# Splitting every second query or key projection of the first phase over two periods, with attention halves and mean products moved behind them

## The reference

```python
Q = (x @ wq + bq).reshape(Bn, Sn, Hn, hd)
K = (x @ wk + bk).reshape(Bn, Sn, Hn, hd)
V = (x @ wv + bv).reshape(Bn, Sn, Hn, hd)
def prep(t):
    h1 = jnp.tanh(jnp.einsum('bshd,do->bsho', t, w1) + b1)
    return jnp.einsum('bsho,on->bshn', h1, w2) + b2
...
qe = jnp.real(jnp.einsum('hcb,bshn->cshn', R, q1))
qq = jnp.sum(qe ** 2, -1)
s = qq[:, :, None, :] * kk[:, None, :, :]
attn = jax.nn.softmax(s / s, axis=2)
out = jnp.einsum('bijh,bjhd->bihd', attn, V).reshape(Bn, Sn, Dn)
return out @ wo + bo
```

## Time and profile before

| | before |
|---|---|
| median of 3 runs | 1529.22 us (1527.8 to 1529.68) |
| the profiled execution | 1528.58 us, span 1526.8 us |
| TensorE busy | 1479.4 us (97%) |
| VectorE busy | 1148.7 us (75%) |
| ScalarE busy | 846.9 us (55%) |
| GpSimd busy | 368.8 us (24%) |

### The profile page before, as it was taken

One profiled execution on the slowest core, in us unless ns is written; L12 is line 12 of the kernel. 1 busy time (PEld: TensorE's weight loads), 2 busy tenths in 40 slices (PEclk: granted clock), 3 DMA queues, 4 the chain that ended last, 5 costly groups with the idle time before them and its releaser, 6 DMA issues.

```text
span 1526.8 us, 28795 instructions
## 1 busy us (share of the span) xinstructions
PE 1479.4 (97%) x11085; PEld 1047.7 (69%) x11085; DVE 1148.7 (75%) x2321; ACT 846.9 (55%) x1123; POOL 368.8 (24%) x404
## 2 busy tenths in 40 slices
PE   9999999999999999999999999999999999999998
PEld 5334343335566666666557888888988888888887
DVE  6545544468999999999967888778786878788676
ACT  5888899866788888888863431322232221222221
POOL 1000000224646666666454300000000000000001
PEclk9999999999999999999999999999999999999999
DMA  7766656457646756656642201100010101110001
GB/s 152 144 112 120 124 99 123 104 87 117 103 68 108 110 74 111 105 81 97 110 143 70 76 15 32 25 28 22 20 30 15 42 14 29 29 29 16 20 22 28
DMA packets 89872, 108.93 MB, mean 71 GB/s; under 512 B 18228, under 2 KB 58176, under 8 KB 89736
## 3 DMA queue, kind: packets, MB, share of 16 engines
q1 hardware_dynamic: 89608, 106.90, 36.9%
q10 hardware_dynamic: 128, 0.20, 0.0%
HBM read 26.29 MB, written 4.19 MB: 20 GB/s over the span
## 4 chain that ended last, share of the span: by engine, by line
PE 73%; DVE 12%; SPq 6%; ACT 3%; issue 3%; DMA 1%; POOL 1%; POOLq 0%; DVEq 0%; ACTq 0%
PE ps L109 70%; SPq L119 6%; DVE NM L1609 2%; PE ps L1382 2%; ACT PX L1550 1%; ACT H L683 1%; DMA XR<-TT 1%; DVE GH L2441 1%; DVE GH L2443 1%; DVE X L2403 1%; DVE TT L2269 1%; PE ps L1344 1%; PE ps L1390 1%; DVE EE L850 1%; ACT GF L2213 1%
## 5 line engine op out<-in xcount | busy, mean ns | idle before, releaser
L1609 DVE TENSOR_REDUCE NM<-ps 128x4 f32<-128x1024 f32 x256 | 307.4, 1220 | 27.3 <-PE ps L109 26.0
L1550 ACT ACTIVATE PX<-ps 128x1024 f32<-128x1024 f32 x256 | 262.2, 1024 | 78.8 <-PE ps L109 77.7
L683 ACT ACTIVATE H<-ps,b1c 128x1024 f32<-128x1024 f32 x256 | 267.6, 1117 | 38.6 <-PE ps L109 37.2
L2213 ACT ACTIVATE GF<-ps,cols 128x512 f32<-128x512 f32 x128 | 87.0, 686 | 257.4 <-PE ps L109 257.4
L109 PE MATMUL ps<-XC,W_sw_w 128*128 128x512 f32 x768 | 187.1, 393 | 0.0
L109 PEld LDWEIGHTS ps<-XC,W_sw_w 128*128 128x128 f32 x768 | 140.0, 188 | 27.6
L2554 POOL TENSOR_SCALAR RSc<-AGc 128x4 f32<-128x4 f32 x23 | 5.6, 243 | 593.9 <-DVE AGc L2328 593.9
L2443 DVE TENSOR_TENSOR GH<-GF,GH 128x512 fp32r<-128x512 f32 x192 | 133.2, 694 | 6.6
L109 PE MATMUL ps<-PX,VT 128*32 128x256 f32 x2048 | 137.1, 385 | 0.1
L2208 ACT ACTIVATE GF<-ps 128x512 f32<-128x512 f32 x64 | 38.1, 596 | 176.2 <-PE ps L109 176.2
L109 PE MATMUL ps<-KT,QT 48*128 48x512 f32 x512 | 127.5, 495 | 2.8 <-DVE NM L1609 1.8
(11 more groups left out here) (254 smaller groups left out, 2507.5 us busy)
## 6 DMA issues: line engine op xcount, KB each, us to landing
KT<-KS SPq DMA_DIRECT2D x128, 192.0 KB, 4.7
ST<-QS SPq DMA_DIRECT2D x254, 96.0 KB, 2.8
QT<-XSb SPq DMA_DIRECT2D x128, 96.0 KB, 4.1
XR<-TT SPq DMA_DIRECT2D x352, 32.0 KB, 1.9
XT<-in_xT_dram SPq DMA_DIRECT2D x8, 512.0 KB, 4.1
raw_a<-in_x_dram SPq DMA_DIRECT2D x8, 512.0 KB, 4.5
CR<-in_ctxT_dram SPq DMA_DIRECT2D x8, 512.0 KB, 4.6
out_dram<-X SPq DMA_DIRECT2D x7, 512.0 KB, 2.9
```

The lines of the kernel that those rows point to most:

```text
L683: e.activation(H1[s % 8][:, :, :], PP[s % 3][:, :, :], ACT.Tanh, bias=b1c[:, half:half + 1], scale=1.0).then_inc(act_th, 1)
L1550: e.activation(PX[s % 3][:, :, :, :], PP[2][:, :, :].rearrange("p g (c q) -> p g c q", c=2), ACT.Exp, bias=0.0, scale=0.25).then_inc(act_e ...
L1609: e.tensor_reduce(NM[u % 2][:, qc, :, :, i], PP[qc][:, :, :].rearrange("p g (m k) -> p g m k", m=2), AX.X, ALU.max, negate=True).then_inc( ...
L2213: e.activation(g[:, :], o, f, bias=cols[:, col:col + 1], scale=1.0).then_inc(act_g, 1)
```

## The change

From J = 35 on, the projection that stands in J = 4n + 3 (J = 35, 39, 43, 47, 51, 55: `halved`) is split. Its first three matmuls (k = 0) stay there, and the last three (k = 1) stand in the next period at the same place, between w1 steps 1 and 2. All that follows from its end moves by one period too: VectorE's two evictions, GpSimd's copy and SP's stack (`projected_due`). To leave bank 7 to the open sum, the rest of the attention halves (J = 40, 48, 56) and the mean product of J = 44 stand behind w2 now, at the end of their period, and the mean vectors of J = 40 and 56 move to the end of J = 41 and 57. On VectorE the reads of these stand behind the projection's eviction.

```diff
+    def halved(J):
+
+        n, t = divmod(J, 4)
+        return t == 3 and n >= DIRECT[0] and n + 2 < NIT
+
+    def projected_due(J):
+
+        if halved(J - 1):
+            return project_due(J - 1)
+        return None if halved(J) else project_due(J)
...
     def means_late_due(J):
-        return {40: 2, 56: 3}.get(J)
+        return {41: 2, 57: 3}.get(J)
...
-        def project(n, c, b, free):
+        def project(n, c, b, free, parts=(0, 1)):
             p, k1 = n // 2, 1 - n % 2
             w.wait_ge(dve_wqk, 4 - 2 * k1)
             w.wait_ge(dve_x, 2 * p + 2)
-            w.wait_ge(*free)
-            for k in range(2):
+            if 0 in parts:
+                w.wait_ge(*free)
+            for k in parts:
...
-            t.then_inc(pe_proj, 1)
+            if 1 in parts:
+                t.then_inc(pe_proj, 1)
...
-            rest = attend_rest_due(J)
-            if rest is not None:
-                free[7] = attend_half(rest, 1, pe_att, free[7])
+            if halved(J - 1):
+                free[7] = project(*project_due(J - 1), 7, free[7], (1,))
...
             if pr is not None and J:
-                free[7] = project(*pr, 7, free[7])
+                free[7] = project(*pr, 7, free[7], (0,) if halved(J) else (0, 1))
...
             m = means2_due(J)
-            if m is not None:
-                b = means2_bank(m)
-                free[b] = means2(m, free[b])
+            if m is not None and means2_bank(m) == 6:
+                free[6] = means2(m, free[6])
...
+            rest = attend_rest_due(J)
+            if rest is not None:
+                free[7] = attend_half(rest, 1, pe_att, free[7])
+            m = means2_due(J)
+            if m is not None and means2_bank(m) == 7:
+                free[7] = means2(m, free[7])
             m = means_late_due(J)
```

More of the change, by code:

```diff
@@ L447, in sync @@
                 dma(e, XM[:, :, :], x_tm[:, 4 * p:4 * p + 4, :], d_xm)
-            pr = project_due(J)
+            pr = projected_due(J)
             if pr is not None:
@@ L828, in centred, with means_rows @@
             t.then_inc(dve_mm, 1)
+        def means_rows(m):
+            w.wait_ge(pe_mb, m + 1)
+            w.wait_ge(pe_att, 2 * m)
+            w.wait_ge(d_bo, 64)
+            e.tensor_tensor(MB[:, :], P[means2_bank(m)][:, 0:256], BO[:, :], ALU.add).then_inc(dve_mb, 1)
         low = P[7][0:48, 0:256]
@@ L856, in vector @@
                     attended(at, u, 6 + u)
-            rest = attend_rest_due(J)
-            if rest is not None:
-                attended(rest, 1, 7)
             if J == SPREAD:
@@ L878, in vector @@
             m = means2_due(J)
[L879 to L884, removed]
+            if m is not None and means2_bank(m) == 6:
+                means_rows(m)
+            pr = projected_due(J)
             if pr is not None:
                 project(*pr, 7)
+            rest = attend_rest_due(J)
+            if rest is not None:
+                attended(rest, 1, 7)
+            m = means2_due(J)
+            if m is not None and means2_bank(m) == 7:
+                means_rows(m)
             if J == BIAS_ROWS:
```

## The result

The changed kernel took **1537.46 us** in the median of 5 runs (1533.82 to 1538.21), the kernel before 1529.22 (1527.8 to 1529.69). The ratio is 1.0049, with a 95% interval of 1.0038 to 1.006: slower by 8.2 us. The forecast was 1528.7 with a range of 1527.0 to 1531.2 and "within 0.2%" at 0.90, so it was wrong in sign and in size. The profiled execution took 1537.66 us.

What follows compares the result with a forecast made beforehand. TensorE was taken to set the pace nearly everywhere. Terms +1.26 - 1.64 - 0.18 + 0.38 + 0 - 0.3 gave -0.5 us, so 1528.1 profiled and a 1528.7 us median, range 1527.0 to 1531.2.

Steps and rivals of the forecast that it cites:

- The mean vector from J=40 to 41: Norms of J=42 may wait for the later centring on VectorE, covered by a 0.27 us stall: counted 0.
- The stacks: Split projections' stacks are issued a period later, but the last still reaches its reader on TensorE in time: 0.
- J=57/58: First maps start 0.98 us earlier in TensorE's work, partly filling J=58's waits, less bank wait and centring: -0.3 us.
- effects further on: Remaining chance of 0.04 for effects further on, making the time either faster or slower.
- A: Rival: halves cost just half of 1.59 us each and waits of J=45 and J=58 are filled: 1526.4 us, chance 0.13.
- B: Rival, slower: the reciprocal in J=43 holds VectorE, delaying the eviction and J=44's mean product; 2.5 us more gives 1531.2, chance 0.13.
- The half projection: Each group of three matmuls takes 0.90 us, so two cost 0.21 more than a whole projection; six splits +1.26 us.
- The stall of J=36: TensorE's 0.82 us wait for ScalarE's tanh is filled by the half projection, also in J=52: -1.64 us.
- The projection of J=41: It waits 0.19 us for VectorE to empty the bank after the attention rest, likewise in J=49: +0.38 us.
- The mean product of J=44: It waits 0.4 us for a late eviction, while J=45's 0.58 us of stalls go: net -0.18 us.

Runs made afterwards that it cites:

- e5: The changed kernel with the projection of J=55 left whole, so the last stack is issued as early as before: 1532.32 us, ratio 1.0023.
- e6: The changed kernel with nine useless matmuls of 128 rows by 512 columns ahead of norms in J=42: 1529.02 us, ratio 1.001.
- e3: The kernel before with only the mean vectors moved to the end of J=41 and 57, nothing split: 1532.13 us, ratio 1.0025.
- e1: The changed kernel with the room for XS doubled, eight columns instead of four: 1529.96 us, ratio 1.0012.
- e7: The changed kernel with both the room for XS doubled and the projection of J=55 left whole: 1528.4 us, ratio 0.9999.
- e10: The kernel before with only the splits of J=35/36 and J=51/52, nothing moved: 1527.56 us, ratio 0.9987.
- e8: The changed kernel with the room for XS doubled and no projection split, the other moves kept: 1531.08 us, ratio 1.0019.
- e9: The changed kernel with one wait added, so GpSimd starts its context tiles only after VectorE's MM: 1531.1 us, ratio 1.0015.
- e4: The changed kernel with useless 48-row matmuls ahead of norms, eight in J=42 and four in J=58: 1533.24 us, ratio 1.0036.
- e2: The changed kernel with the mean vectors back at the end of J=40 and 56: 1533.64 us, ratio 1.0031.

## Why the prediction was wrong

**The step that failed** is "The mean vector from J=40 to 41 ... I count 0, bounds -0.27 and +0.5". The order of VectorE's instructions was read rightly ("behind the eviction, XS and the normalisation of J=41"), but I took XS as ready to run, since in the trace of before it ran directly behind the eviction. It has a wait for the mean vector itself, which the mean vector's old place had always met. The price was 1.99 us for the wait alone (`e5`, `e6`), and 4.64 (8.64 against 4.00) with the fallen clock in the profiled execution. `e3` shows this with that line alone, `e1` by taking it away.

**A second step failed**, "The stacks ... 0" together with J=57/58. I asked whether the late stack would reach its reader on TensorE in time, and it did. What I didn't ask is beside what GpSimd's work would now run. The trace of before had the answer in a row that I used for something else: the gains took 1.23 us and had started at 296.87, 0.06 us behind a GpSimd subtraction (296.81, 1.28 us); in `e7` the same operation started at 296.03, 0.07 us ahead of GpSimd's (296.10), and took 0.22. The Trainium skill ("SBUF — State Buffer", section "Who interferes with whom") states it as a rule: a VectorE instruction with two SBUF inputs contends with a GpSimd instruction that reads SBUF, since its second input comes through a read interface that both share. The rows here agree: 1.68 and 1.86 us beside a subtraction of 1.3 us, 0.52 without. Price 1.33 us, and 3.78 with the clock.

**What was left out altogether** is the granted clock. The forecast added up work and waits at full speed; each of the two waits, of 2.20 and 0.96 us, was followed in the profile by a stretch at half clock that cost 2.65 and 2.45 us more, over half of the loss at both places. A chance of 0.04 "for effects further on" was all I had left for such things. The profiled difference, by first tanhs, comes out as +2.0 (the clock at 42 us, which the kernel before didn't have in its profile), +4.6 (J=42), +3.3 (J=58) and -0.8 for the rest, 9.1 us, so some 7 us of that execution are the change's. The medians differ by 8.2, and the least of the five runs, 1533.82, lies 4.6 above the median of before.

**The rivals.** A (halves free) did not come: groups of three were 0.90 us long throughout (190.60 to 191.50 in `e10`). B named the wrong instruction, the reciprocal in J=43, though the right kind of thing, VectorE held by one wait with the bank's eviction behind it.

**The terms that held**, read in `e7` where nothing ahead disturbs them. The half projection costs 0.90. The stall of J=36 is gone: with both halves counted, J=35 and 36 take 0.63 us less (forecast 0.82 - 0.21 = 0.61). The projection of J=41 waits for X: 0.95 us from w1 to it (216.83 to 217.78), 0.29 more than w1's 0.66, where 0.19 was forecast. The mean product of J=44 was to wait 0.4 us for the eviction behind the reciprocal and waited 0.35. From the first tanh of J=35 to that of J=53 `e7` gained 0.36 us; by the forecast's terms (-1.64, -0.18, +0.38 and five splits at 0.21) it was to be 0.39.

**The term for J=57/58**, "I take -0.3, bounds -0.98 and +0.3", is to be read in `e1`, which has all six splits and no meeting of the two engines. From J=54 to J=59 it took 25.66 us against 25.98 before, 0.32 less; by the forecast's terms, -0.3 and one split at 0.21, it was to be 0.09 less. Part of that is luck: the gains took 0.22 us instead of 1.23, for the reason above, which the forecast did not have. From J=35 to J=63 `e1` gained 0.64 us in its profile, where the forecast's sum says 0.5. `e7` gained nothing from J=35 to J=63: with its last projection whole, the attention rest that was moved leaves a stall of 0.74 us in J=56, as in J=40 of `e8`. So the small terms were right and didn't matter, since two steps that I had set to zero, without looking at the waits behind them, carried the result. That `e7`'s median, 1528.4, is near the forecast of 1528.7 says little, as the kernel before is as near.

**What stays open.** Why the clock falls behind the wait of J=42 in one execution (after, `e3`, `e9`) and not in another with the same instructions (`e5`) was not settled. That it depends on the matmuls ahead is not shown: `e4` and `e6` point that way, but they differ in the number of rows and in the operands, and `e6` kept its clock behind the unfilled wait of J=58 too. Why the median of `e1` is 1.8 us above the kernel before, when its profile is shorter over the changed periods, is open as well. What `e10` would gain with the room for XS doubled as well wasn't run.

## What to carry to other kernels

When an instruction is moved later, list who waits for its semaphore, those that only wait to reuse a buffer too, since in the old trace they wait for nothing and leave no row; then ask what stands behind each of them in its engine's order. A stall that is filled is worth its length at most, so compare it with the price of a new wait, which here was its length plus, in several profiles, as much again or more in fallen clock. Split or move only where the trace has a stall: two splits out of six, with nothing moved, gave the only version whose interval lies below the kernel before.

## What the runs showed of the hardware

- A wait of TensorE of 0.9 to 2.2 us ahead of small groups was followed in several executions by a granted clock of one half: for 6.8 us at 226.8 and at 305.3 (after), for 3.4 us at 219.2 (`e2`) and at 226.2 (`e9`). At half clock w2 takes 3.57 us instead of 1.86. The same wait as at 226.8 left the clock at 1.00 in `e5`, and so did one of 1.14 us in J=58 of `e6`, longer than the 0.96 of the kernel after.
- With eight more matmuls of 48 rows in that wait, which left some 0.9 us of it empty, the clock was 0.50 in the one traced execution, the slowest of five; with nine of 128 rows, which filled it, it was 1.00 in the one traced.
- Part of the spread between executions of one kernel goes with this: the five of the kernel after had mean clocks of 0.993, 0.993, 0.994, 0.996 and 0.996 and took 1537.66, 1538.21, 1537.46, 1533.82 and 1535.26 us; `e5` took 1530.1 at 0.998 and 1534.12 at 0.995. The fall at 42 us, in unchanged code, is in the profiles of `e4`, `e5`, `e8` and the kernel after and not in the others. With the longer wait ahead of it, 1.85 to 1.95 us against 1.49 before, it costs about 2 us; `e1` and `e3` had waits of 1.92 and 1.91 there and no fall, and lost 0.4.
- VectorE's four small products (MM) took 1.68 and 1.86 us beside a GpSimd subtraction of 1.3 us, and 0.52 without it. For the gains operation a start 0.13 us earlier against GpSimd's decided between 0.22 and 1.23 us.
- A group of three 128 x 512 matmuls took 0.90 us and one of six 1.59 from start to start, both between w1 groups, in this phase too: each group has a price of its own of about 0.2 us.
